# Feed forward stage with ternary weights stationary for gate and up, and the inner layer left untransposed

## The chip, the cores and the metric

One core of a Trainium2 chip runs the whole program. The metric is the device time of one execution in microseconds, which lasts as long as that core is at work. TensorE (PE in the rows, its weight loads PEld), VectorE (DVE), ScalarE (ACT), GpSimd (POOL) and SyncE (SP, which here only issues DMAs) each work through their own list of instructions in order and meet at semaphores.

## The reference

1600 tokens (16 sequences of 100) of 512 values go through one block: cross attention (16 heads of 128, 361 context positions of 256 values), then a feed forward layer with 1.58 bit weights. The diff touches only the second half:

```
x = x + xattn(layernorm(x), ctx)                # its last product, with Wo, is done in the third stage
n = layernorm(x)
h_bitlinear(a, w) = act_quant(fwht(a)) @ weight_quant(w).T
  fwht:         normalised Walsh-Hadamard transform along the last axis
  act_quant:    s = 127 / max|row|;  clip(round(a * s), -128, 127) / s
  weight_quant: s = mean|w|;         clip(round(w / s), -1, 1) * s
x = x + h_bitlinear(silu(h_bitlinear(n, w_gate)) * h_bitlinear(n, w_up), w_down)
```

w_gate and w_up are 2048 x 512, w_down is 512 x 2048. The inner layer of a token has 2048 values, and its Hadamard transform has that length.

## The kernel before

Three stages run one after the other: `queries`, `attention` and `feed_forward`. The first two leave the attention's output, transposed, in DRAM (`o_dram`). The third, which is all that changes, goes over the tokens in tiles of 128: 12 whole tiles and one of 64 (`TILES` is 13). Each engine has a list `step(i)`, written out by hand, and `pipeline` runs it for i = -2 to 12. A step works on several tiles at once: the down product of tile i, the inner layer of tile i+1, the output projection and the norm of tile i+2, and the loads and first projections of tile i+3.

For one tile t the data goes this way:

- SyncE's `load_o` (L1349) brings the attention output of the tile into the single buffer `o_in`, transposed, 1024 KB. `load_x` (L1361) brings the residual into the single buffer `x_in`; it waits for the sum x1 of the tile before. In step i SyncE issues, in this order: the two DMA transposes of q2 (`turn_q2`), load_x(i+3), load_o(i+4), and the store of the result (`store`).
- `high_o` (ScalarE, L1682) rounds o_in to the matmul's format, and `low_o` (GpSimd, L1428) makes the remainder. `out_proj` (TensorE, L1491) multiplies them with Wo: 16 heads, three matmuls each (high x high, high x low, low x high), 512 columns. AHEAD = 6 heads of a tile are done in the step before, the other 10 behind gate and up.
- `residual` (VectorE, L1811 to L1818) adds x, giving x1, and takes mean and variance; `inverse_deviation` (GpSimd) makes the power; `norm` and `rotate_halves` (L1824, L1832) follow. `norm_T` transposes into psA, `high_xT` (ScalarE, L1709) and `low_xT` (VectorE, L1836) split it, and `rotate_in` (TensorE, L1513) multiplies with a 256 x 256 Hadamard matrix, giving token rows in psF.
- `scales1` takes the maximum of the rows, `round1` and `ints1` make 8 bit integers, `q1_T` (L1524) transposes them, and `copy_q1T` (L1729) brings them to SBUF.
- `gate_up(t, j)` for four blocks j of 512 inner values: q1T is the stationary operand, the 8 bit ternary weights `wt` are the moving one, 512 columns at a time (L1542), so that the tokens are on the partitions. Silu (ScalarE, L1743) takes gate's scale as its per-partition scale, and `hidden` (VectorE, L1898) multiplies with up and its scale.
- The Hadamard transform of the 2048 inner values is partly done with sums and differences, on VectorE (L1907, L1914, L1920) and on GpSimd (L1447, L1450, L1456), within `hid` and `half_rot`. The rest takes a Hadamard matrix of 256: `hidden_T` (TensorE, L1588) transposes each block, `high_hT` (ScalarE, L1689) and `low_hT` (VectorE, L1801) split it out of PSUM, and `rotate_hidden` (L1598) multiplies.
- `peak`, `scales2`, `round2` and `ints2` make the integers q2, a DMA turns them, and `down` (L1608) gives psF, which `scale_down` (ScalarE, L1735) scales and `result` (GpSimd, L1461) adds to x1.

In `step`, ScalarE's order behind the four Silus is high_hT 0 and 1, high_o(i+3), scale_down(i), high_hT 2 and 3, high_xT(i+2), round1, round2, copy_q1T, round2. VectorE's is residual(i+2), low_hT 0, norm, rotation, low_hT 1, peak 0 and so on. GpSimd's is rotate_pair0, rotate_across, inverse_deviation, low_o(i+3), result(i), move_residuals. The half tile has versions of its own (`gate_up_halves`, `hidden_T_halves`, `cross_halves`), and TensorE fills pauses with matmuls that nobody reads (`busy`, L1616).

Of the kernel before, what the change touches and what calls it, by code (L numbers as in the profile page):

```python
# [14 lines left out]
F32 = mybir.dt.float32  # L15
# [38 lines left out]
def build(nc, x, ctxT, ctx_k, wq, wk, wv, wo, gq, gk, w_ff, ident_in, had_in, out):  # L54
# [4 lines left out]
    with ExitStack() as top:  # L59
# [10 lines left out]
        passed = {e: sem(e + "_passed") for e in ("sp", "act", "dve", "pe")}  # L70
# [1183 lines left out]
def feed_forward(nc, sbt, sem, passed, bank0, ident, neg_half, w127, o_in, d_stored, d_first, x, x_in, xT0, wo_hi, wo_lo, had_in, o_dram,  # L1254
# [10 lines left out]
    with ExitStack() as ctx:  # L1265
# [13 lines left out]
        al, ald = sb("al", [P, 2]), sb("ald", [P, 1])  # L1279
# [21 lines left out]
        p_out, p_xT, p_rx, p_q1T, p_gu, p_hT, p_rh, p_down = (  # L1301
            s(f"p3_{n}") for n in ("out", "xT", "rx", "q1T", "gu", "hT", "rh", "down"))
# [5 lines left out]
        a_q1T, a_sil, v_h, g_pair0, v_pair1, v_r2, g_r2 = (s(n) for n in ("a3_q1T", "a3_sil", "v3_h", "g3_pair0", "v3_pair1",  # L1308
                                                                                  "v3_r2", "g3_r2"))
        v_cross, a_half = s("v3_cross"), s("a3_half")  # L1310
# [4 lines left out]
        AHEAD, FIRST = 6, 10  # L1315
# [22 lines left out]
        def _(sp):  # L1338
# [78 lines left out]
        def _(pool):  # L1417
# [22 lines left out]
            def rotate_pair0(t):  # L1440

                pool.wait_ge(v_h, t * NB + 2)
                if due(t * NB):
                    pool.wait_ge(p_hT, t * NB)
# [7 lines left out]
            def rotate_across(t):  # L1452
# [3 lines left out]
                nc.gpsimd.tensor_tensor(half_rot[:, 2:4, :], hid[:, 0:2, :], hid[:, 2:4, :], op=ALU.subtract).then_inc(g_r2, 1)  # L1456

            def result(t):
                pool.wait_ge(a_y, t + 1)
                pool.wait_ge(g_old, (t + 2) * 2)  # L1460
                nc.gpsimd.tensor_tensor(y[:], y[:], x1[:, 0, :], op=ALU.add).then_inc(g_y, 1)  # L1461

            def step(i):
                if real(i + 1) and not last_tile(i + 1):
# [4 lines left out]
                if real(i + 3) and not (isinstance(i, int) and i == -2):  # L1469
                    low_o(i + 3)  # L1470
# [8 lines left out]
        def _(pe):  # L1479
            def out_proj(t, heads):  # L1480
                first = isinstance(t, int) and t == 1
                if heads[0] == 0:
                    if not first:
                        pe.wait_ge(g_o, t - 1)
                        pe.wait_ge(v_xT, t - 1)
                for h in heads:
                    if first:
                        pe.wait_ge(v_o, h // OH + 1)
# [6 lines left out]

            def norm_T(t):
                pe.wait_ge(v_xr, t * 2)
                for c in range(DC):
                    last = nc.tensor.transpose(psA[:, c * P:(c + 1) * P], xr[:, c * P:(c + 1) * P], ident[:])
# [17 lines left out]
            def q1_T(t):  # L1517
# [3 lines left out]
                if due(t * NB):  # L1521
                    pe.wait_ge(v_hT, t * NB)
                for c in range(DC):
                    last = nc.tensor.transpose(psTb[1][:, c * P:(c + 1) * P], q1[:, c * P:(c + 1) * P], ident_b[:])  # L1524
                last.then_inc(p_q1T, 1)

            def gate_up(t, j):
# [18 lines left out]
            def gate_up_halves(t, j):  # L1546

                if j == 0:
                    pe.wait_ge(a_q1T, t + 1)
                pe.wait_ge(a_mag[1], 2 * t - 1 + j)  # L1550
                pe.wait_ge(v_h, t * NB + j - 1)
                apart(pe, pe_passed)
                for k in range(2):
                    for c in range(DC):
                        for g in range(2):
                            col = (j + g * NB // 2) * DIM
                            last = nc.tensor.matmul(psB[g * TH:(g + 1) * TH, 2 * j + k, :], q1T[:, c, g * TH:(g + 1) * TH],  # L1557
                                                    wt[:, k, c, col:col + DIM], start=(c == 0), stop=(c == DC - 1),
                                                    tile_position=(0, g * TH))
                last.then_inc(p_gu, 1)  # L1560

            def hidden_T_halves(t, n):
                pe.wait_ge(v_pair1, t * 6 + 5 + n)
                pe.wait_ge(a_q1T, t + 1)
                for c in range(DC):
                    last = nc.tensor.transpose(psT[n][:, c * P:(c + 1) * P], hid[:, n, c * P:(c + 1) * P], ident[:])  # L1566
                last.then_inc(p_hT, 1)
# [11 lines left out]

            def hidden_T(t, n):  # L1580
                if n % 2 == 0:
                    pe.wait_ge(g_r2 if n else v_r2, t + 1)
                if n < 2:
                    pe.wait_ge(a_q1T, t + 1)
                else:
                    pe.wait_ge(v_hT, t * NB + n - 1)
# [470 lines left out]
```

## Time and profile before

| | us |
|---|---|
| three runs: median (lowest, highest) | 1415.81 (1414.24, 1416.08) |
| the profiled execution: span | 1415.7 |
| TensorE busy in the span | 1384.3 (98%) |
| VectorE, ScalarE, GpSimd busy | 933.8 (66%), 940.2 (66%), 517.2 (37%) |
| one step of the third stage, first gate/up matmul to the next | 29.14 |

The span runs from the first instruction to the last of one profiled execution. Busy time is the time for which an engine had an instruction under way; TensorE's matmuls overlap, so the distance between the starts of two matmuls tells what one costs, not its length. The third stage begins at about 1029 us of the span.

### The profile page before, as it was taken

The page shows a single profiled execution, that of the slowest core. Times are in us where ns is not written, and L with a number is a line of the kernel's source. Part 1 is how long each engine was busy: PE and PEld are TensorE (multiplying, and loading weights), DVE is VectorE, ACT ScalarE, POOL GpSimd, SP SyncE. Part 2 cuts the span into 40 slices and gives each one's busy share as a digit, 9 for nine tenths or more (in the row PEclk, how much of TensorE's full clock was granted, in tenths as well). Part 3 has the DMA queues.
Part 4 walks back from the last instruction along what each step waited for, and adds up shares of the span by engine and source line. Part 5 has one row for each costly group of instructions (what it writes and reads, how often), then busy time and mean ns, then how long its engine had stood idle before and what let it go on. Part 6 is the DMA issues. An engine that isn't in the chain of part 4 may idle for free. (4 is left out here: it accounts for less than half of the span.)

```text
span 1415.7 us, 25806 instructions
## 1 busy us (share of the span) xinstructions
PE 1384.3 (98%) x8407; PEld 1192.2 (84%) x8407; DVE 933.8 (66%) x2399; ACT 940.2 (66%) x2072; POOL 517.2 (37%) x323
## 2 busy tenths in 40 slices
PE   8999988999999999999999999999989999999998
PEld 8889867999999999999999999998867677776775
DVE  5222036667777777777777777766457677776775
ACT  4566558888888888888888888887533433343332
POOL 0033324432233223332323332324645465655551
PEclk9999999999999999999999999999989999999999
DMA  6867823334443443444344344325443322233211
GB/s 219 215 189 220 226 54 91 100 111 117 128 112 114 134 128 114 116 124 134 107 124 117 113 133 128 106 82 172 126 153 79 86 60 67 61 97 75 60 30 42
DMA packets 173492, 165.05 MB, mean 117 GB/s; under 512 B 81440, under 2 KB 149040, under 8 KB 171568
## 3 DMA queue, kind: packets, MB, share of 16 engines
q1 hardware_dynamic: 166448, 150.82, 38.5%
q10 hardware_dynamic: 6912, 12.59, 2.7%
q8 instruction: 69, 1.13, 0.3%
q14 instruction: 63, 0.52, 0.1%
HBM read 123.44 MB, written 33.01 MB: 111 GB/s over the span
## 5 line engine op out<-in xcount | busy, mean ns | idle before, releaser
L764 POOL TENSOR_TENSOR rk_sp<-ms_sp,neg_half 76x10 f32<-76x10 f32 (+1 forms) x128 | 238.5, 1880 | 567.0 <-DMA ms_sp<-ms 567.0
L1194 DVE CUSTOM_DVE_ANT_0 sc<-psS,rk 100x361 f32<-100x361 f32 x256 | 136.4, 533 | 97.1 <-PE psS L839 71.3
L986 ACT ACTIVATE pr<-ex,ri 100x361 f32<-100x361 f32 x256 | 153.6, 600 | 63.6 <-DVE ri L1184 63.6
L979 ACT ACTIVATE ex<-sc,nb,rq_all 100x361 f32<-100x361 f32 x256 | 175.9, 687 | 7.8 <-DVE nb L1203 7.8
L867 PE MATMUL psZ<-pT_hi,cK_hi 120*128 120x400 f32 (+1 forms) x384 | 133.3, 347 | 0.0
L867 PE MATMUL psZ<-pT_hi,cK_lo 120*128 120x400 f32 (+1 forms) x384 | 132.4, 345 | 0.0
L867 PE MATMUL psZ<-pT_lo,cK_hi 120*128 120x400 f32 (+1 forms) x384 | 132.2, 344 | 0.0
L852 PEld LDWEIGHTS psP<-ident,pr 100*120 100x120 f32 (+1 forms) x768 | 80.2, 165 | 43.5 <-issue 35.3
L839 PE MATMUL psS<-ring_hi,q_hi 128*100 128x362 f32 x256 | 97.0, 379 | 5.0 <-DVE mx L1194 5.0
L852 PE MATMUL psP<-ident,pr 100*120 100x100 f32 (+1 forms) x768 | 96.5, 261 | 4.0 <-ACT pr L986 4.0
L1176 DVE TENSOR_TENSOR pT_lo<-psP,pT_hi 121x600 fp32r<-121x600 f32 x128 | 99.0, 773 | 1.5 <-ACT pT_hi L1010 1.5
L882 PE MATMUL psNV<-z,wv_sb 128*128 128x200 f32 x504 | 97.2, 336 | 0.8 <-issue 0.8
L1184 DVE RECIPROCAL ri<-rs 100x1 f32<-100x1 f32 x256 | 41.3, 161 | 85.5 <-ACT ex L979 81.5
L1689 ACT ACTIVATE hT_hi<-psT 128x512 fp32r<-128x512 f32 x48 | 27.5, 596 | 99.8 <-PE psT L1588 99.8
L961 ACT ACTIVATE ring_hi<-bank 128x362 fp32r<-128x362 f32 x128 | 60.6, 473 | 44.1 <-PE bank L815 42.6
L1542 PE MATMUL psB<-wt,q1T 128*128 128x512 fp8e4 x384 | 86.6, 379 | 0.0
L815 PE MATMUL bank<-cT_hi,wk_hi 128*128 128x362 f32 x256 | 85.3, 333 | 1.0 <-DVE ring_lo L1129 1.0
L815 PE MATMUL psK<-cT_hi,wk_hi 128*128 128x362 f32 x256 | 85.0, 332 | 0.7 <-DVE ring_lo L1129 0.7
L1010 ACT ACTIVATE pT_hi<-psP 121x600 fp32r<-121x600 f32 x128 | 84.7, 662 | 0.0
L882 PEld LDWEIGHTS psNV<-z,wv_sb 128*128 128x128 f32 x504 | 83.0, 190 | 1.2 <-issue 1.1
L839 PE MATMUL psS<-ring_hi,q_lo 128*100 128x362 f32 x256 | 84.0, 328 | 0.0
L839 PE MATMUL psS<-ring_lo,q_hi 128*100 128x362 f32 x256 | 83.9, 328 | 0.0
(295 smaller groups left out, 3947.6 us busy)
## 6 DMA issues: line engine op xcount, KB each, us to landing
rk<-rk_dram SPq DMA_DIRECT2D x64, 564.1 KB
q_dram<-q_out SPq DMA_DIRECT2D x64, 200.0 KB, 4.3
q_in<-q_dram SPq DMA_DIRECT2D x64, 200.0 KB, 5.2
o_dram<-o SPq DMA_DIRECT2D x64, 200.0 KB, 5.4
stage<-in_w_ff SPq DMA_DIRECT2D x12, 1024.0 KB, 6.3
w_in<-in_w_ff ACTq DMA_DIRECT2D x48, 256.0 KB, 2.4
o_in<-o_dram SPq DMA_DIRECT2D x12, 1024.0 KB, 5.9
cT_in<-in_ctxT SPq DMA_DIRECT2D x15, 361.0 KB, 5.4
```

The lines of the kernel that those rows point to most:

```text
L764: nc.gpsimd.tensor_tensor(rk_sp[:, cols], ms_sp[:, cols], neg_half[0:HG * SKR, :].to_broadcast([HG * SKR, n]), op=ALU.pow).then_inc(g_rk, 1)
L815: last = nc.tensor.matmul(psK[h % 2][:, 0:SKP], w[:, c, col:col + D], x[:, slot, c, :], start=(n == 0), stop=(n == 3 * CC - 1))
L839: last = nc.tensor.matmul(psS[0:SQ, 0:SKP], w[:, u % 2, cols], x[:, u % NG, h, :], start=(i == 0), stop=(i == 2))
L852: last = nc.tensor.transpose(psP[0:KW[i], k, i * SQ:(i + 1) * SQ], pr[:, 2 * half + k, KO[i]:KO[i] + KW[i]], ident[0:SQ, 0:SQ])
L867: last = nc.tensor.matmul(psZ[c][:, 0:UQ], w[0:KW[i], b % 2, i, c * P:(c + 1) * P], x[0:KW[i], u % 2, i, :], start=(n == 0), stop=(n == 8))
L882: last = nc.tensor.matmul(bank[:, k * 2 * SQ:(k + 1) * 2 * SQ], wv_sb[:, c, col:col + D], z[:, first % 4:first % 4 + 2, c, h * SQ:(h + 1) ...
L979: nc.scalar.activation(ex[:, h % 2, :], sc[:, h % 2, :], ACT.Exp, bias=nb[:, h % 2:h % 2 + 1], scale=factor(n), accum_out=rs[:, h % 2:h % ...
L986: nc.scalar.activation(pr[:, h, :], ex[:, h % 2, :], ACT.Copy, scale=ri[:, h % 2:h % 2 + 1]).then_inc(a_pr, 1)
L1010: nc.scalar.activation(two_heads(pT_hi, u, half), psP[0:KW[0], :, 0:3 * SQ].rearrange("p k (i q) -> p k i q", q=SQ), ACT.Copy).then_inc(a_ ...
L1176: nc.vector.tensor_tensor(two_heads(pT_lo, u, half), psP[0:KW[0], :, 0:3 * SQ].rearrange("p k (i q) -> p k i q", q=SQ), two_heads(pT_hi, u ...
L1194: nc.vector.tensor_tensor_reduce(out=sc[:, h % 2, :], in0=psS[0:SQ, 0:SK], in1=rk[:, u % 2, h, :], scale=1.0, scalar=-3.0e38, op0=ALU.mult ...
L1542: last = nc.tensor.matmul(psB[:, 2 * (j % 2) + k, :], q1T[:, c, :], wt[:, k, c, j * DIM:(j + 1) * DIM], start=(c == 0), stop=(c == DC - 1))
```

## The change

Gate and up are computed with the ternary weights as the stationary operand, in pieces of 128 x 128, and the transposed integers q1T as the moving one, 128 columns at a time. The inner values come out on the partitions and the tokens along the columns, so `hidden_T` and its halves version go away, and high_hT and low_hT read `half_rot` in SBUF. Gate's scale is now one per column: `scales1` spreads it over a row of 128 (`al_rows`), TensorE transposes that (`al_T`), ScalarE copies it (`copy_alT`), and VectorE multiplies each gate block with it (`gate`) ahead of Silu. Up's scale is put off to `scales2`. The head products are split into `out_high` (both high parts, 10 heads ahead of time) and `out_low`, and low_o moves from the end of a step of GpSimd (tile i+3) to the start of the next (tile i+2). SyncE loads o for tile i+3 instead of i+4. All waits of the passing marks share one semaphore.

```diff
@@ sync, step
-            load_o(3, 3 * TT)
...
                 if real(i + 3):
                     load_x(held(sp, i + 3), held(sp, start(i + 3)))
-                if real(i + 4):
-                    load_o(held(sp, i + 4), held(sp, start(i + 4)))
+                if real(i + 3):
+                    load_o(held(sp, i + 3), held(sp, start(i + 3)))
                 store(i, held(sp, start(i)))
@@ gpsimd
             def low_o(t):
                 pool.wait_ge(a_o, t + (NO - 1))
-                pool.wait_ge(v_xr, 2 * t - 2)
+                pool.wait_ge(v_q[1], 2 * t - 2)
...
-                nc.gpsimd.tensor_tensor(half_rot[:, 2:4, :], hid[:, 0:2, :], hid[:, 2:4, :], op=ALU.subtract).then_inc(g_r2, 1)
+                for n in range(2):
+                    nc.gpsimd.tensor_tensor(half_rot[:, 2 + n, :], hid[:, n, :], hid[:, 2 + n, :], op=ALU.subtract).then_inc(g_r2, 1)
             def result(t):
                 pool.wait_ge(a_y, t + 1)
+                pool.wait_ge(v_hT, t * NB + (NB + NB // 2 if isinstance(t, int) and t == TILES - 2 else 2 * NB))
...
             def step(i):
+                if real(i + 2) and not (isinstance(i, int) and i < 0):
+                    low_o(i + 2)
                 if real(i + 1) and not last_tile(i + 1):
                     rotate_pair0(i + 1)
                     rotate_across(i + 1)
                 if real(i + 2) and i > -2:
                     inverse_deviation(i + 2)
-                if real(i + 3) and not (isinstance(i, int) and i == -2):
-                    low_o(i + 3)
@@ tensor
+            def out_high(t, heads):
+                if heads[0] == 0:
+                    pe.wait_ge(a_o, t + (NO - 1))
+                    pe.wait_ge(v_x1, t - 1)
+                for h in heads:
+                    for w in (wo_hi, wo_lo):
+                        nc.tensor.matmul(psA[:], o_hi[:, h, :], w[h // HALF][:, h % HALF, :], ...)
+            def out_low(t):
+                pe.wait_ge(g_o, t - 1)
+                for h in range(H):
+                    last = nc.tensor.matmul(psA[:], o_lo[:, h, :], wo_hi[h // HALF][:, h % HALF, :], ...)
+                last.then_inc(p_out, 1)
+            def al_T(t):
+                pe.wait_ge(v_scale[0], 6 * t + 6)
+                nc.tensor.transpose(psT[0][:, 0:TT], al_rows[:], ident[:]).then_inc(p_alT, 1)
@@ gate_up
-                for k in range(2):
-                    for c in range(DC):
-                        last = nc.tensor.matmul(psB[:, 2 * (j % 2) + k, :], q1T[:, c, :],
-                                                wt[:, k, c, j * DIM:(j + 1) * DIM], start=(c == 0), stop=(c == DC - 1))
-                last.then_inc(p_gu, 1)
+                width, chunks = (TH, FC // 2) if last_tile(t) else (TT, FC // NB)
+                for k, done in enumerate((p_gate, p_up)):
+                    for i in range(chunks):
+                        col = (j * chunks + i) * P
+                        for c in range(DC):
+                            last = nc.tensor.matmul(psB[:, 2 * (j % 2) + k, i * width:(i + 1) * width], wt[:, k, c, col:col + P],
+                                                    q1T[:, c, 0:width], start=(c == 0), stop=(c == DC - 1))
+                    last.then_inc(done, 1)
@@ tensor, step behind gate and up (hidden_T gone)
+                    out_high(i + 2, range(AHEAD, H))          # AHEAD = 10
+                    out_low(i + 2)
                     down(i, 0, front)
                     down(i, 1, front)
+                    rotate_hidden(i + 1, 0), (1), (2)
                     norm_T(i + 2)
                     rotate_hidden(i + 1, 3)
+                    out_high(i + 3, range(0, 1))
                     rotate_in(i + 2)
+                    out_high(i + 3, range(1, 7))
                     q1_T(i + 2)
+                    al_T(i + 2)
+                    out_high(i + 3, range(7, AHEAD))
@@ scalar, step
+                    silu(i + 1, j)                             # for each j; in place in sil
+                    high_hT(i + 1, n)                          # all four, from half_rot
                     high_o(i + 3)
                     scale_down(i)
                     high_xT(i + 2)
                     round1(i + 2); round2(i + 1, 0); copy_q1T(i + 2)
+                    copy_alT(i + 2)
                     round2(i + 1, 1)
@@ vector
+            def gate(t, j):
+                dve.wait_ge(p_gate, t * NB + j + 1)
+                dve.wait_ge(a_alT, t + 1)
+                nc.vector.tensor_tensor(sil[:, j % 2, :], psB[:, 2 * (j % 2), :], alT (repeated), ALU.mult).then_inc(v_g, 1)
             def hidden(t, j):
-                nc.vector.scalar_tensor_tensor(hid[:, j, :], psB[:, 2 * (j % 2) + 1, :], al[:, 1:2], sil[:, j % 2, :], ...)
+                nc.vector.tensor_tensor(hid[:, j, :], psB[:, 2 * (j % 2) + 1, :], sil[:, j % 2, :], ALU.mult).then_inc(v_h, 1)
@@ vector, step
+                    gate(n), hidden(n) for n in 0, 1, 2; gate(3), rotate_within(2), hidden(3), rotate_within(3)
+                    low_hT(0); residual(i + 2); low_hT(1); low_hT(2); norm; rotate_halves; low_hT(3); peak(0); low_xT(i + 2)
+                    peak(1), peak(2), peak(3); scales1(i + 2); scales2(i + 1)
```

## Rows read from the trace of the kernel before

**Rows 1.** The page, busy time of each engine and granted clock in 40 slices

```profile
PE 1384.3 (98%) x8407; PEld 1192.2 (84%) x8407; DVE 933.8 (66%) x2399; ACT 940.2 (66%) x2072; POOL 517.2 (37%) x323
...
PEclk9999999999999999999999999999989999999999
```

**Rows 2.** Groups of TensorE in 960 to 1416: busy us, mean ns, idle before

```profile
L1542 PE MATMUL psB<-wt,q1T 128*128 128x512 fp8e4 x384 | 86.6, 379 | 0.0
...
L1588 PE MATMUL psT<-ident,stage 128*128 128x128 f32 x192 | 28.1, 281 | 2.5 <-DVE stage L1920 2.5
```

**Rows 3.** TensorE in order of time, one step: start us, length us

```profile
1157.07 7.22 PE L1542 MATMUL psB<-wt,q1T 128*128 128x512 fp8e4 x32
1163.94 0.58 PE L1491 MATMUL bank<-wk_hi,o_hi 128*128 128x512 f32 x1
...
1171.12 1.03 PE L1588 MATMUL psT<-ident,stage 128*128 128x128 f32 x8
1171.99 3.62 PE L1608 MATMUL psF<-wt,q2T 128*128 128x512 fp8e4 x16
...
1184.52 0.40 PE L1524 MATMUL psT<-ident_b,q 128*128 128x128 bf16 x4
...
1186.21 7.22 PE L1542 MATMUL psB<-wt,q1T 128*128 128x512 fp8e4 x32
```

**Rows 4.** Busy time of each engine in one step

```profile
1157.07:1186.21 29.14, 29.11 (x161) 20.61 (x161) 21.35 (x40) 11.32 (x16) 16.31 (x10) 1.00 0.29 73
```

**Rows 5.** VectorE in order of time, the step from 1186.21

```profile
1186.68 0.69 DVE L1876 TENSOR_SCALAR q<-mag 128x1024 bf16<-128x1024 f32 x1 [0.80 <-ACT mag L1721]
...
1192.51 0.75 DVE L1898 SCALAR_TENSOR_TENSOR stage<-psB,al,sil 128x512 f32<-128x512 f32 x1 [1.11 <-ACT sil L1743]
1193.30 2.40 DVE L1907 TENSOR_TENSOR stage<-stage 128x256 f32<-128x256 f32 x2
...
1198.84 1.23 DVE L1920 TENSOR_TENSOR stage<-stage 128x1024 f32<-128x1024 f32 x1
1200.45 0.69 DVE L1811 TENSOR_TENSOR x<-bank,x_in 128x512 f32<-128x512 f32 x1 [0.39 <-PE bank L1491]
```

**Rows 6.** SyncE in order of time, the same step

```profile
1201.17 0.34 SPq L1361 DMA_DIRECT2D x_in<-in_x  x1
1209.20 0.37 SPq L1349 DMA_DIRECT2D o_in<-o_dram  x1
```

**Rows 7.** The loads of o, issue to landing, 1100 to 1300

```profile
DMA to landing us min/median/max: 5.8/5.9/6.0
```

**Rows 8.** ScalarE in order of time, the conversion of o

```profile
1201.86 1.91 ACT L1682 ACTIVATE o_hi<-o_in 128x2048 fp32r<-128x2048 f32 x1
```

**Rows 9.** Line L1524: ns min/median/max, first and last start

```profile
L1524 PE MATMUL psT<-ident_b,q x52: 219/219/230, 1039.1 to 1388.7; 128*128 128x128 bf16 x52
```

**Rows 10.** Line L1783

```profile
L1783 ACT ACTIVATE o_hi<-o_in x4: 611/616/632, 1028.9 to 1030.5; 128x512 fp32r<-128x512 f32 x4
```

**Rows 11.** Line L1907

```profile
L1907 DVE TENSOR_TENSOR stage<-stage x52: 409/740/1509, 1047.3 to 1395.4; 128x256 f32<-128x256 f32 x52
```

**Rows 12.** Line L1447

```profile
L1447 POOL TENSOR_TENSOR stage<-stage x24: 1264/1272/1289, 1045.6 to 1367.6; 128x512 f32<-128x512 f32 x24
```

**Rows 13.** Busy time and granted clock at the stage's start

```profile
1027.30:1030.60 3.30, 1.42 (x5) 0.93 (x6) 1.38 (x2) 2.28 (x6) 1.62 (x2) 1.00 0.40 122
1030.60:1034.00 3.40, 3.40 (x12) 2.86 (x12) 2.21 (x5) 2.01 (x4) 0.77 (x2) 0.50 0.97 321
1051.10:1054.50 3.40, 0.88 (x6) 0.45 (x5) 3.33 (x6) 0.00 (x0) 1.53 (x1) 1.00 0.00 0
1054.50:1061.30 6.80, 6.08 (x30) 5.67 (x29) 5.08 (x11) 3.59 (x4) 5.26 (x3) 0.50 0.12 39
```

**Rows 14.** TensorE in order of time, the last tile

```profile
1389.83 3.64 PE L1557 MATMUL psB<-wt,q1T 128*64 128x512 fp8e4 x32 [0.87 <-ACT q1T L1729]
...
1400.13 0.38 PE L1598 MATMUL psB<-had,hT_hi 128*128 128x256 f32 x1 [0.49 <-DVE hT_lo L1941]
```

More of the change, by code:

```diff
@@ L1300, in feed_forward @@
         a_o, v_o, g_o = s("a3_o"), s("v3_o"), s("g3_o")
-        p_out, p_xT, p_rx, p_q1T, p_gu, p_hT, p_rh, p_down = (
-            s(f"p3_{n}") for n in ("out", "xT", "rx", "q1T", "gu", "hT", "rh", "down"))
+        p_out, p_xT, p_rx, p_q1T, p_alT, p_gate, p_up, p_rh, p_down = (
+            s(f"p3_{n}") for n in ("out", "xT", "rx", "q1T", "alT", "gate", "up", "rh", "down"))
         v_x1, v_st, g_rs, v_xn, v_xr = (s(n) for n in ("v3_x1", "v3_st", "g3_rs", "v3_xn", "v3_xr"))
@@ L1479, in _, with first_out_proj @@
         def _(pe):
[L1480 to L1485, printed above, removed]
+            def first_out_proj(heads):
                 for h in heads:
-                    if first:
-                        pe.wait_ge(v_o, h // OH + 1)
+                    pe.wait_ge(v_o, h // OH + 1)
                     hi, lo = (w[h // HALF][:, h % HALF, :] for w in (wo_hi, wo_lo))
@@ L1494, in out_proj @@
                     last.then_inc(p_out, 1)
+            def out_high(t, heads):
[4 more added lines that the diff above has]
+                    for w in (wo_hi, wo_lo):
+                        nc.tensor.matmul(psA[:], o_hi[:, h, :], w[h // HALF][:, h % HALF, :],
+                                         start=(h == 0 and w is wo_hi), stop=False)
+            def out_low(t):
+                pe.wait_ge(g_o, t - 1)
+                for h in range(H):
+                    last = nc.tensor.matmul(psA[:], o_lo[:, h, :], wo_hi[h // HALF][:, h % HALF, :],
+                                            start=False, stop=(h == H - 1))
+                last.then_inc(p_out, 1)
             def norm_T(t):
                 pe.wait_ge(v_xr, t * 2)
+                pe.wait_ge(a_alT, t)
                 for c in range(DC):
-                    last = nc.tensor.transpose(psA[:, c * P:(c + 1) * P], xr[:, c * P:(c + 1) * P], ident[:])
+                    last = nc.tensor.transpose(psT[0][:, c * P:(c + 1) * P], xr[:, c * P:(c + 1) * P], ident[:])
                 last.then_inc(p_xT, 1)
@@ L1578, in down_halves @@
                 last.then_inc(p_down, 1)
[L1580 to L1586, printed above, removed]
-                for c in range(DC):
-                    last = nc.tensor.transpose(psT[n % 2][:, c * P:(c + 1) * P], half_rot[:, n, c * P:(c + 1) * P], ident[:])
-                last.then_inc(p_hT, 1)
             def rotate_hidden(t, n):
@@ L1644, in step @@
                         gate_up(i + 1, j)
-                if real(i + 2):
-                    out_proj(i + 2, range(FIRST if isinstance(i, int) and i == -1 else AHEAD, H))
-                if real(i + 1):
-                    hidden_T(i + 1, 0)
-                    hidden_T(i + 1, 1)
+                if isinstance(i, int) and i == -1:
+                    first_out_proj(range(FIRST, H))
+                elif real(i + 2):
+                    out_high(i + 2, range(AHEAD, H))
+                    out_low(i + 2)
                 if real(i):
@@ L1684, in high_hT @@
             def high_hT(t, n):
-                act.wait_ge(p_hT, t * NB + n + 1)
+                if last_tile(t):
+                    act.wait_ge(v_r2, t + 2)
+                else:
+                    act.wait_ge(g_r2, 2 * t + (n - 1)) if n >= 2 else act.wait_ge(v_r2, t + 1)
                 if n == 0:
@@ L1708, in high_xT @@
                     act.wait_ge(p_rx, t)
[L1709 removed]
+                nc.scalar.activation(xT_hi[:].rearrange("p c t -> p (c t)"), psT[0][:], ACT.Copy).then_inc(a_xT, 1)
             def round1(t):
[L1712 removed]
+                act.wait_ge(v_scale[0], 6 * t + 4)
                 if due(t):
@@ L1966, in step @@
                 if i == TILES - 2:
+                    gate(i + 1, 0)
                     hidden(i + 1, 0)
+                    gate(i + 1, 1)
                     rotate_within(i + 1, 0)
@@ L1983, in step @@
                     for n in range(3):
+                        gate(i + 1, n)
                         hidden(i + 1, n)
+                    gate(i + 1, 3)
                     rotate_within(i + 1, 2)
@@ L1999, in step @@
                     return
+                if real(i + 1):
+                    low_hT(i + 1, 0)
                 if real(i + 2):
@@ L2002, in step @@
                 if real(i + 1):
-                    low_hT(i + 1, 0)
+                    low_hT(i + 1, 1)
+                    low_hT(i + 1, 2)
                 if real(i + 2):
@@ L2015, in step @@
                 if real(i + 1):
-                    peak(i + 1, 2)
-                    peak(i + 1, 3)
+                    for n in range(1, NB):
+                        peak(i + 1, n)
                 if real(i + 2):
```

219 lines of the change are left out of this document (90 added, 129 removed).

## The prediction

> **What bounds the kernel now.** I read first the head of the page: TensorE is busy 98% of the span, at full clock almost throughout [rows 1]. Then the groups by line over the last third, the feed forward stage, since the diff touches only that stage: TensorE's matmul groups there show no idle time ahead of them but for 2.5 us once, and the transposes of the inner layer, L1588, are 192 matmuls, 16 for each of 12 tiles [rows 2]. Then TensorE in order of time over one step of the tile loop [rows 3]: its first gate/up matmul starts at 1157.07 and again at 1186.21, so a step takes 29.14 us. TensorE is busy 29.11 of it [rows 4], so the stage is bound by TensorE. Below, "+t" is the time in a step after its first gate/up matmul.
>
> How much room the others have decides this change. In the same row VectorE is busy 21.35, ScalarE 11.32, GpSimd 16.31. VectorE's landmarks [rows 5], against the step that starts at 1186.21: the rotation across blocks ends at +13.9, the residual sum x1 runs +14.2 to +14.9. SyncE [rows 6] issues x_in at +15.0 (it waits for x1) and o_in at +23.0. An o_in takes 5.9 us from issue to landing [rows 7], so it is there at about +28.9; the conversion that reads it, o_hi on ScalarE, 1.91 long [rows 8], runs at +15.7 of the NEXT step. It is a load with 16 us to spare.
>
> **The change, part by part.**
>
> TensorE's own work. Out go 16 transposes a step at L1588; eight of them take 1171.12 to 1171.99, 0.109 each [rows 3], so 1.74. Gate and up keep their 16384 moving columns, now as 128 matmuls of 128 columns instead of 32 of 512. The old ones pass in 6.87 [rows 3]. No row shows an 8 bit stationary operand. Nearest is L1524, a bf16 128x128 stationary with 128 columns: four end 0.40 after the first starts [rows 3], one lasts 0.219 [rows 9], so (0.40-0.22)/3 = 0.060 apart; a quarter of the old 0.215 is 0.054. I take 0.056, so 7.15, +0.28. The upper end is the f32 transposes' 0.109, so 13.95, +7.1. Below 0.054 nothing can be had, since the columns alone take that. The transpose of the scales adds one at 0.109. The head matmuls are the same 48, in another order. If nothing waited: 29.14-1.74+0.28+0.11 = 27.8 a step.
>
> The Trainium skill's page TensorE: Matmul & The Clock Gate, section Back-to-back issue gap, says that a real stream of weight load and matmul pairs at 128 columns runs at about 81 ns a pair, not at 56. No run of 128 such pairs is in this trace. By that rule gate and up would take 10.4, an estimate from the page.
>
> VectorE. Gate's scale now lies along the columns, so each block gets a multiply out of PSUM before Silu: 4 x 0.69 (x1, L1811, is the same shape and kinds of operand [rows 5]). The up product loses its scalar: 0.75 to 0.69, -0.24. The scale rows, 128 elements: +0.2. Together +2.7: 24.1 a step. Within a block the chain is now gate multiply 0.69, Silu 0.62 (the 512 element o_hi copy from SBUF, L1783 [rows 10]), up product 0.69: 2.0 a block, and it runs once for each of four blocks, since VectorE's next gate multiply is behind the up product. VectorE gets to the first one at +1.25, behind the integers of the tile before it (L1876, 1186.68 and 0.69 long, [rows 5]). So three blocks are done at 7.3 and the fourth gate multiply at +7.9; in before, the third product ended at +7.05. From there the order is the old one: 2.2 for the first half rotation beside GpSimd, 0.6 product, 1.2, 1.2 and 1.2, the rotation across ends at +14.3, half a microsecond later than now. TensorE doesn't feel that: it comes to the rotation of block 0 at 7.15+2.96 (12 high head matmuls)+3.73 (16 low ones)+3.45 (down) = +17.3.
>
> low_hT now reads two operands from SBUF. L1907, the half rotation of 256 elements, takes 0.41 at best and 1.51 at worst [rows 11], and its long pair, 2.40, lies beside GpSimd's work [rows 5]: I read it as each waiting till the other's instruction ends. GpSimd's cross subtraction, now two instructions of 512 elements at 1.27 [rows 12], starts with VectorE's at +13.1, and the first ends at +15.4. So: ScalarE's hT_hi ends at +15.0, low_hT of block 0 is held till +15.4 and ends at +16.1. It stands ahead of the residual in the new order, so x1 ends at +16.7, 1.8 later than now. If it were not held and the chain were short, x1's floor is the end of the low head matmuls, +14.0, plus 0.7.
>
> **The step I think decides: o_in.** low_o of GpSimd moves from the end of a step to the start of the next, and with it SyncE's load of o goes from tile i+4 to tile i+3, behind load_x, in the same step in which ScalarE's high_o(i+3) reads it. load_x waits for x1. So x1 +16.7, x_in's issue 0.35, o_in issued at +17.1, landed 5.9 later at +23.0, where 28.9 was good before. Behind high_o's wait on ScalarE stand: the scaling of down, xT_hi, both roundings and the copy of q1T. Nothing of them may pass. I walk on, with 0.6 for a pass over 512 elements on ScalarE [rows 10] and 0.7 on VectorE [rows 5]: high_o 1.91, ends +24.9; scaling 0.6, +25.5; xT_hi 0.6, +26.0; low_xT on VectorE 0.7, +26.7; rotate_in on TensorE 0.95 and 0.2 to arrive, +27.9; the peaks 1 to 3, queued behind low_xT, end at +28.5; the maximum and the scale 1.2, +29.7; round1 0.7, +30.4; VectorE finishes the second scale and makes the integers, +31.0; q1's transposes 0.2, the copy behind the first round2, +32.2; TensorE has by then three heads to finish, till +32.8. So a step takes 32.8. Walked with the same rules, the old order gives 29.0 and x1's end at +14.95, which is what the trace has (29.14, +14.9); so the walk is good to 0.2.
>
> TensorE then stands still where it waits for high_o (+21.9 to +24.9, 3.0), for low_xT (1.35), and for q1 (0.6), together 5.0; it does 27.8 of work. Cost without anything else: 32.8-29.1 = 3.7 in each of the ten steps 0 to 9 that convert an o tile behind a load: +37.
>
> The clock. At the start of the stage TensorE was busy 1.42 of 3.30 us, and then the granted clock is 0.50 (1.2 GHz) for 3.4 us; later 0.88 of 3.40, and then it is 0.50 for 6.8 [rows 13]. Those are idle times of 1.9 and 2.5, and every new step has 3.0 and 1.35 within 5 us. In each new step I expect a half clock stretch of 3.4 us, in rotate_in and the head matmuls behind it: half of it, 1.7, is lost, less the 0.4 or so of the 0.6 pause that it fills: +1.3 a step, +13. If the stretch is 6.8: 3.4 less 0.6, +28. None: 0.
>
> The rest. The step before the loop (gate and up of tile 0) had a pause of 2.5; it loses the transposes but TensorE now waits at the rotation, which starts at about +16.1 against +16.3: 0, +-2. Step 10 has no o load: -1.3. The last tile: 128 matmuls of 64 columns against 32 in 3.64 now [rows 14]; two gate multiplies (1.4) go in, the transposes, the copies and the PSUM sums between go out for quarter sums of 1.5 and 1.3; the rotation can start at about +10.4 against +10.3 now [rows 14]. 0, up to +2. The query and attention stages run the same instructions: 0. One shared semaphore for the passing marks costs nothing, since nobody waits on it.
>
> Sum: the profiled execution's time is its span, 1415.7, against a median of 1415.8. 1415.7+37+13-1.3 = 1464.
>
> **Rivals.**
> (a) The load binds but the clock holds, or x1 comes earlier. 1415.7+37-1 = 1452; with x1 at its floor of +14.7 each step is 2.0 shorter, 1432. For it: the pauses are split. Against: rows 13 show a fall after 1.9 alone. 25%.
> (b) Stationary loads don't keep up with 128 columns. At 0.109 gate and up end at +13.95; walking on gives a step of 37.7, 1415.7+10x8.5+5 (the other two steps and the last tile) = 1506: 6%. Half way between 0.056 and 0.109, at 0.082, the step is 34.2, with ten times 5.1 and 7 for the other three: 1473: 7%. For both: only four such pairs in a row are in the trace. Against: they were 0.060 apart. The half way case is about what the Trainium skill's TensorE: Matmul & The Clock Gate, section Back-to-back issue gap, has as the rule (81 ns).
> (c) VectorE's two-input instructions are held more than I walked, each low_hT once by 1.3 of GpSimd: x1 1.3 later, blocks 1 to 3 later: 1475. For: L1907's 1.51. Against: the result's new wait keeps GpSimd off. 7%.
> (d) The other side, faster. If o_in were ready, the walk gives 28.5 (VectorE's chain through x and q1 ends last, 0.7 over TensorE's 27.8): 11 x -0.6 = 1409; without that chain 11 x -1.37 = 1401. It decides from the point where o_in lands by about +19.3: a landing in 2.2 us instead of 5.9, or an issue before +13.4, ahead of the end of the head matmuls, which load_x forbids. The loads of the steady steps took 5.8 to 6.0 [rows 7]. 5%.
> (e) Gains and losses cancel, within 0.2%, which is about what a measurement here tells from nothing: 3%.
> (f) My own case, with the clock falling in most steps: 47%.
>
> Together: faster 0.05, same 0.03, slower 0.92. Range: (a) without its floor, (f) with 6.8 us stretches in half the steps, (c) and half of (b): 1440 to 1486.
>
> **What would show it.** In the changed kernel's trace: the first gate/up matmuls of two steps 33 to 34 apart; gate and up in 7.2; o_in issued near +17 and landed near +23, and high_o right behind it, named as the releaser of a TensorE pause of about 3; x1 ending near +16.7; granted clock of 0.50 once a step; GpSimd's result waiting till +25. Wrong if o_in's issue is not tied to x1, if high_o has no idle time ahead of it, if gate/up matmuls are 0.08 or more apart, or if steps take less than 29.

## The result, and the profile after

The changed kernel takes 1473.4 us (median; 1472.6 to 1477.8) beside 1415.1 for the kernel before on the same chip: a ratio of 1.042, interval [1.041, 1.043]. The profiled execution took 1473.3, its span is 1471.5.

The page, engines' busy time and the slices of TensorE's busy share and clock, against [rows 1]:

```profile
PE 1392.0 (95%) x9468; PEld 1235.6 (84%) x9468; DVE 961.8 (65%) x2462; ACT 941.5 (64%) x2083; POOL 526.6 (36%) x335
...
PE   8999989999999999999999999998888888888887
...
PEclk9999999999999999999999999999899999999999
```

TensorE's busy time rose by only 8 us, the span by 56; its share fell from 98% to 95%, and the slices in which it fell are all at the end, in the feed forward stage. (The page's own chain says little here: it reaches back only through the last tile. The waits have to be read by window.)

The first gate/up matmul of each tile gives the steps. They were 29.1 us long [rows 3]; now they start at 1037.2, 1067.1, 1102.3, 1136.8, 1171.6, 1207.7, 1242.4, 1276.8, 1311.1, 1345.2, 1379.3, 1416.4 and 1444.8. The ten steps that convert an o tile behind its load take 35.1, 34.5, 34.8, 36.1, 34.7, 34.5, 34.3, 34.1, 34.2 and 37.1, together 57.9 more than ten old ones. The rest is small: the step before them +0.56, the one behind them -0.35, the last tile +0.8, and the stages ahead of this one -3.1. The change doesn't touch those stages, and they differ by more than that from one execution to the next: in the profiled executions of e1 to e9 below, this stage starts anywhere from 1035.1 to 1045.5 (before's had a stretch at half clock at 13.5 us). Sum: +55.8, which is the difference of the spans, 1471.5 - 1415.7.

The groups of TensorE in 980 to 1474, against [rows 2]; behind the bar busy us, mean ns, and the idle time ahead with what ended it:

```profile
L1565 PE MATMUL psB<-q1T,wt 128*128 128x128 bf16 (+1 forms) x1664 | 92.6, 217 | 0.8 <-ACT q1T L1713 0.8
L1587 PE MATMUL psB<-had,hT_hi 128*128 128x256 f32 x200 | 55.7, 312 | 10.1 <-DVE hT_lo L1778 10.1
...
L1497 PE MATMUL bank<-wk_hi,o_hi 128*128 128x512 f32 x88 | 46.2, 525 | 32.8 <-ACT o_hi L1670 32.8
...
L1526 PE MATMUL psF<-had,xT_hi 128*128 128x256 f32 x48 | 19.9, 422 | 8.1 <-DVE xT_lo L1812 8.1
```

From the first gate/up matmul on, TensorE's idle times come to 54 us, where before has 5.7, and 33 of them end with o_hi. The mean of L1497 with wk_hi, 525 ns, where the same matmuls with ring_hi take 403, is already the second effect: many of them run at half clock. (The mean of L1565, 217, is a matmul's length from end to end of the array, not its distance from the next.)

Who waits for whom, 1040 to 1430 (us in total, times, longest):

```profile
POOL y L1461 <- ACT y L1719: 72.0, 10, 9.1
...
ACT o_hi L1670 <- DMA o_in<-o_dram: 57.1, 10, 7.6
...
PE bank L1497 <- ACT o_hi L1670: 32.8, 10, 5.2
...
PE psB L1587 <- DVE hT_lo L1778: 8.0, 12, 4.2
PE psF L1526 <- DVE xT_lo L1812: 7.8, 10, 1.1
```

Ten times, once in each long step, ScalarE waits for the o tile, and TensorE for ScalarE.

One such step in order of time, from 1207.68, put together from the engines' timelines. TensorE, against [rows 3]:

```profile
1207.68 7.39 PE L1565 MATMUL psB<-q1T,wt 128*128 128x128 bf16 x128
...
1221.40 3.63 PE L1597 MATMUL psF<-wt,q2T 128*128 128x512 fp8e4 x16
...
1226.30 0.39 PE L1587 MATMUL psB<-had,hT_hi 128*128 128x256 f32 x1 [0.32 <-DVE hT_lo L1778]
...
1232.78 0.79 PE L1497 MATMUL bank<-wk_hi,o_hi 128*128 128x512 f32 x1 [2.80 <-ACT o_hi L1670]
...
1234.57 0.58 PE L1526 MATMUL psF<-had,xT_hi 128*128 128x256 f32 x1 [0.57 <-DVE xT_lo L1812]
1234.95 0.41 PE L1526 MATMUL psF<-had,xT_lo 128*128 128x256 f32 x1
```

VectorE, against [rows 5]:

```profile
1222.82 0.98 DVE L1778 TENSOR_TENSOR hT_lo<-stage,hT_hi 128x512 fp32r<-128x512 f32 x1 [0.70 <-ACT hT_hi L1680]
1223.72 0.68 DVE L1787 TENSOR_TENSOR x<-bank,x_in 128x512 f32<-128x512 f32 x1
```

SyncE, against [rows 6], and the landings of six o loads, against [rows 7]:

```profile
1224.43 0.34 SPq L1360 DMA_DIRECT2D x_in<-in_x  x1
1224.87 0.38 SPq L1348 DMA_DIRECT2D o_in<-o_dram  x1
```

```profile
DMA to landing us min/median/max: 5.9/6.0/7.0
```

ScalarE and GpSimd, against [rows 8]:

```profile
1230.81 1.91 ACT L1670 ACTIVATE o_hi<-o_in 128x2048 fp32r<-128x2048 f32 x1 [5.22 <-DMA o_in<-o_dram]
```

```profile
1233.38 1.27 POOL L1461 TENSOR_TENSOR y<-y,x 128x512 f32<-128x512 f32 x1 [6.73 <-ACT y L1719]
```

Read it from the VectorE row on: low_hT of block 0 is 0.98 long where the others take 0.68 (GpSimd's instruction that writes half_rot runs beside it until +15.6; I read it as held by that), x1 ends at +16.7, x_in and behind it o_in are issued at +16.7 and +17.2, o_hi starts at +23.1 and ends at +25.0, TensorE goes on at +25.1 after a pause of 2.8, and GpSimd's result has waited 6.7 for the scaling behind o_hi.

The busy time of this step, of the pause, and of what follows it (PE, PEld, DVE, ACT, POOL, granted clock), against [rows 4]:

```profile
1207.68:1242.40 34.72, 31.03 (x243) 25.06 (x243) 23.55 (x45) 11.52 (x17) 17.22 (x11) 0.90 0.24 59
...
1232.60:1239.40 6.80, 6.05 (x17) 4.69 (x18) 5.00 (x16) 2.22 (x5) 2.50 (x3) 0.50 0.10 39
```

The granted clock is 0.50, the lower of its two levels, for 6.8 us from the end of the pause. So the pause is paid twice: 2.8 us of standing still, and then rotate_in and the head matmuls at half speed.

### The profile page after: what moved, and what is told of

Read it like the earlier page. It is cut to its first block and busy times, and to the rows that moved or that the text cites. A ratio compares the mean times of both kernels' runs of the same rounds, so it can differ in the third digit from the quotient of the medians.

```text
span 1471.5 us, 28072 instructions
## 1 busy us (share of the span) xinstructions
PE 1392.0 (95%) x9468; PEld 1235.6 (84%) x9468; DVE 961.8 (65%) x2462; ACT 941.5 (64%) x2083; POOL 526.6 (36%) x335
## 5 line engine op out<-in xcount | busy, mean ns | idle before, releaser
L1565 PEld LDWEIGHTS psB<-q1T,wt 128*128 128x128 fp8e4 x1664 | 89.8, 98 | 5.0 <-issue 4.2
L1565 PE MATMUL psB<-q1T,wt 128*128 128x128 bf16 (+1 forms) x1664 | 92.6, 217 | 0.8 <-ACT q1T L1713 0.8
L1680 ACT ACTIVATE hT_hi<-stage 128x512 fp32r<-128x512 f32 x50 | 29.9, 626 | 86.8 <-DVE stage L1913 69.8
L815 PE MATMUL psK<-cT_hi,wk_lo 128*128 128x362 f32 x256 | 83.9, 328 | 0.0
```

Of the source, the lines that this page charges most:

```text
L815: last = nc.tensor.matmul(psK[h % 2][:, 0:SKP], w[:, c, col:col + D], x[:, slot, c, :], start=(n == 0), stop=(n == 3 * CC - 1))
L1565: last = nc.tensor.matmul(psB[:, 2 * (j % 2) + k, i * width:(i + 1) * width], wt[:, k, c, col:col + P], q1T[:, c, 0:width], start=(c == 0) ...
```

## Experiments

"After" is the changed kernel. Each time stands beside the kernel before on the same chip: 1413.7 for the first four, 1414.9 for e5 to e7, 1415.1 for e8 and e9. The theory: the o load, whose issue now stands behind x1, sets the step, and the clock's fall behind its pause is a second, smaller price. The rivals: the new gate/up form or VectorE's longer work costs the time and the load is incidental.

**e1: the load of o ahead of the load of x, nothing else.**

```
 step(i) of SyncE, after:
-    load_x(i + 3)
     load_o(i + 3)
+    load_x(i + 3)
```

> The changed kernel with one pair of lines swapped: in SyncE's step the load of o stands ahead of load_x, so it waits only for low_o of the tile before (GpSimd, over at about +5.8 of a step) and no longer for the residual sum x1 (+16.6). Theory (the load of o, issued behind x1, is what lengthens the step): o_in is issued near +6, lands near +12, high_o runs right behind high_hT at +18 to +20, TensorE's pause of 3.9 us for o_hi goes, and with it the falls of the clock; the step goes from 34.9 to 28.5 us and the kernel to 1473-10x6.4 = 1409, a little faster than the kernel before (about 0.995). What ends last is then VectorE's chain to the integers of q1, with about 0.6 of pause at q1's transposes; at 27.8 (1402) TensorE alone would bind. Rival A (VectorE's extra 2.7 us of work and its waits for GpSimd's port use carry the loss): the step falls by less than 2 us, to 33 or more, and the kernel stays above 1450. Rival B (the stationary weights cost more than their rows say): gate and up stay long and the kernel stays above 1430.

Measured: 1413.0 us, ratio 0.9994 [0.9982, 1.0007]: all 58 us are gone (I had 1409), with 128 gate/up matmuls, the gate multiplies and the new orders of GpSimd and VectorE in place. SyncE in one step (from 1180.90), and the step's busy times:

```profile
1186.94 0.38 SPq L1348 DMA_DIRECT2D o_in<-o_dram  x1
1197.72 0.33 SPq L1360 DMA_DIRECT2D x_in<-in_x  x1
...
1198.80 1.90 ACT L1670 ACTIVATE o_hi<-o_in 128x2048 fp32r<-128x2048 f32 x1
```

```profile
1180.90:1209.90 29.00, 28.11 (x243) 22.95 (x243) 23.46 (x45) 11.39 (x17) 17.25 (x11) 1.00 0.30 74
```

o_in is issued at +6.0, and o_hi has no idle time ahead of it. The step is 28.96, a little above the 28.5 that I had for it. What is left is two short waits of TensorE in each step (1070 to 1380):

```profile
PE psT L1537 <- DVE q L1859: 5.4, 10, 0.6
...
PE psB L1587 <- DVE hT_lo L1778: 3.9, 11, 0.5
```

**e2: the old kernel with the late load alone.** No other part of the change is in it.

```
 SyncE, before:
-    load_o(3, 3 * TT)            # ahead of the loop
 step(i):
     load_x(i + 3)
-    load_o(i + 4)
+    load_o(i + 3)
```

> The kernel before with only SyncE's order of the change: o is loaded for tile i+3 behind load_x(i+3) instead of for tile i+4; nothing else is changed. Theory: this alone is worth as much as the whole change or more. x1 ends at +14.9, o_in is issued at +15.4, lands 7 later at +22.4, high_o ends at +24.3 and the second pair of high_hT stands behind it; low_o on GpSimd (4.6) follows it, and the first head matmuls of tile i+3 wait for low_o. A step of 33.5 at full clock, 35 to 36 with the falls of the clock, against 29.14: 1415+10x5.9 = 1474, between 1458 and 1486. Rival A (the other parts of the change carry the loss): within 10 us of the kernel before, under 1425.

Measured: 1469.0, ratio 1.038 [1.036, 1.041]. In the old kernel the load alone costs 55 us, where the whole change costs 58. SyncE and ScalarE in one step, from 1204.34 (x1 ends at +14.9):

```profile
1219.74 0.38 SPq L1349 DMA_DIRECT2D o_in<-o_dram  x1
...
1226.42 1.91 ACT L1681 ACTIVATE o_hi<-o_in 128x2048 fp32r<-128x2048 f32 x1 [6.32 <-DMA o_in<-o_dram]
```

It fits the theory and adds something: x1 is 1.8 earlier than in after and o_hi starts at +21.3 to +22.2 in nine of the ten steps, and yet the steps are as long (34.0 to 34.8 in eight of them). Those eight end 12.4 to 12.9 behind o_hi's start, where after has 10.8 to 12.0. The old order of ScalarE and TensorE puts more of the inner layer behind the wait.

**e3: after, with work for TensorE in the pause.** Fifteen matmuls that nobody reads, to hold the clock.

```
 step(i) of TensorE:
     rotate_hidden(i + 1, 3)
+    busy(psT[1], 15)
     out_high(i + 3, range(0, 1))
```

> The changed kernel with 15 matmuls that nobody reads (512 columns, 0.23 us each, 3.4 together) in TensorE's pause ahead of the first head matmuls of tile i+3. The wait is as long as before, the engine only isn't idle in it. Theory: the granted clock then stays at 2.4 GHz in the steps, rotate_in takes 0.95 instead of 1.9 and the head matmuls 0.23 instead of 0.43; the step goes from 34.9 to about 33.7, the kernel to 1473-12 = 1461 (1455 to 1466). Rival (the falls of the clock are hidden by the wait for the integers, which ends the pause at q1's transposes anyway): unchanged within 3 us. If the fillers run past the landing they cost: then above 1475.

Measured: 1464.4, ratio 1.035 [1.033, 1.037]; the granted clock is 1.00 throughout a step, and the step 33.2:

```profile
1202.70:1235.80 33.10, 31.57 (x257) 25.68 (x256) 23.46 (x45) 11.31 (x17) 17.23 (x11) 1.00 0.30 65
```

```profile
1224.87 3.59 PE L1605 MATMUL psT<-wk_hi 128*128 128x512 f32 x15
```

(I had 33.7 for the step and 1461 in all.) Its steps give the cleanest rule of the case. In nine steps from 1068.8 on, o_hi starts at +23.21, 23.27, 24.06, 23.34, 23.14, 23.15, 23.07, 23.26, 23.22 in a step and the steps are 33.20, 33.28, 34.07, 33.34, 33.14, 33.17, 33.09, 33.27, 33.23: with the clock held, a step is o_hi's start and 10.0. (The walk had +23.0 and 32.8, so 9.8.) Ten steps come to 336.1, against 349.3 in after: the clock costs 13 of the 58 us. The median fell by only 9: the filling also runs in the step before the loop, where nothing has to be filled (32.4 for 29.9), and the profiled execution, 1461.8, was the fastest of four.

**e4: after, with x1 ahead of low_hT of block 0 on VectorE.**

```
-    low_hT(i + 1, 0)
     residual(i + 2)
+    low_hT(i + 1, 0)
```

> The changed kernel with residual(i+2) ahead of low_hT(i+1, 0) on VectorE. x1 then ends at +15.0 to +15.2 instead of +16.6, and x_in and o_in are issued 1.5 earlier. Theory (the step is a loop through x1 and the load): the step gets shorter by about the same 1.5 us, less what the clock makes of it, and the kernel goes to 1473-15 = 1458 (1453 to 1466). Rival A (the rotation of block 0, which waits for low_hT(0) and now comes 1.5 later, sets the step): unchanged or slower. Rival B (the load's own time isn't bound to x1): unchanged.

Measured: 1450.4, ratio 1.025 [1.023, 1.027]. One step, from 1131.13, with x1 ending at +15.1:

```profile
1145.55 0.68 DVE L1787 TENSOR_TENSOR x<-bank,x_in 128x512 f32<-128x512 f32 x1
...
1146.71 0.41 SPq L1348 DMA_DIRECT2D o_in<-o_dram  x1
...
1153.49 1.91 ACT L1670 ACTIVATE o_hi<-o_in 128x2048 fp32r<-128x2048 f32 x1 [4.83 <-DMA o_in<-o_dram]
```

More than I expected (23 us, not 7 to 20): the nine steps ahead of the last are 31.4 to 33.5, and in six of them the clock falls, in three it doesn't. x1's place counts as long as the load hangs on it.

**e6: after, o ahead of x but still behind x1**, so that only x_in's 0.43 us on the queue is taken away.

```
 step(i) of SyncE, after:
+    sp.wait_ge(v_x1, i + 2)
+    load_o(i + 3)
     load_x(i + 3)
-    load_o(i + 3)
```

> The changed kernel with the load of o still behind x1 but issued ahead of load_x instead of behind it (a wait for x1 stands ahead of both). Theory (o_in landed 7.0 us after its issue and not 5.9, since x_in is moved at the same time just ahead of it, and its issue itself took 1.4 instead of 0.4): o_in lands 0.4 (x_in's issue) and 1.1 earlier, near +22.5 of a step instead of +24.0; the step gets 1.5 shorter, the kernel 1473-15 = 1458 (1453 to 1466). Rival (the landing is slower for another reason, the step's other traffic): only the 0.4 is won, 1469.

Measured: 1469.4, ratio 1.037 [1.035, 1.040]. My number was 1458; the rival's 1469 held. o_hi does start 0.5 earlier (+22.7 in most steps), but half of the steps are 34.1 to 34.3 as in after: in six steps the clock's fall lasts 6.8 us, and such a step is o_hi's start and 11.4 to 11.7. So the wait for x1 is what makes e1's gain, not the order of the two loads.

**e7: e1 without the gate multiplies.** Silu reads gate unscaled out of PSUM, so the scale of gate is left out of the result.

```
-    gate(i + 1, n)                                       # VectorE, four a tile
-    nc.scalar.activation(sil[:, j % 2, :], sil[:, j % 2, :], ACT.Silu)
+    nc.scalar.activation(sil[:, j % 2, :], psB[:, 2 * (j % 2), :], ACT.Silu)
     # ... and the waits of Silu and copy_alT that belong to them
```

> The kernel with the load of o ahead of load_x (step 28.96) and without VectorE's four multiplies of gate with its scales: Silu reads the gate block out of PSUM unscaled, so the result is not the reference's. It asks where the 1.4 us of a step that TensorE no longer works (16 transposes less, 0.4 more for gate and up and the scales) went. Theory (into VectorE's chain, whose end, the integers of q1, TensorE waits for: four multiplies of 0.6 and the wait for them ahead of Silu): x1 ends about 1.5 earlier, the pauses ahead of the rotations and q1's transposes go, the step goes to 28.0 and the kernel to 1413-9 = 1404 (1401 to 1407). Rival (the step is held by the waits for GpSimd's instructions or by gate and up themselves): 28.8 or more, above 1410.

Measured: 1412.1, ratio 0.998 [0.996, 0.999]; a step 28.83 against 28.96. I had 28.0 and 1404: this theory fell. But the run takes less from VectorE than its edit says. The four multiplies were 2.7 us a step; VectorE's busy time fell only from 23.46 to 22.65, and x1 ends at +16.65 instead of +16.8. The half rotations (L1900), which now start at +6.3 instead of +7.9 and lie beside GpSimd's own rotations throughout, took 5.0 us a step instead of 3.5. The line in e1 and in e7 (ns min/median/max, 1070 to 1380):

```profile
L1900 DVE TENSOR_TENSOR stage<-stage x44: 410/793/1518, 1072.8 to 1366.2; 128x256 f32<-128x256 f32 x44
```

```profile
L1900 DVE TENSOR_TENSOR stage<-stage x44: 799/1346/1517, 1080.9 to 1373.1; 128x256 f32<-128x256 f32 x44
```

So e7 doesn't tell what a lighter VectorE would bring; it tells that the gate multiplies cost next to nothing where they stand. The wait ahead of q1's transposes is what it was (1070 to 1380):

```profile
PE psT L1537 <- DVE q L1859: 5.9, 11, 0.5
```

It ends a chain that begins with TensorE itself: rotate_in, maximum, scale, round1, integers, 3.3 to 3.4 us, against the matmuls of six heads, 2.7 us, that lie beside it. Some 0.4 of the chain is VectorE's order: in e1's step from 1180.9 the last matmul of rotate_in ends at +23.9, and the maximum of its result starts at +24.4, right behind three peaks of the inner layer.

**e5: e1, with x1 first, and one head more ahead of q1's transposes.**

```
 TensorE:  out_high(i + 3, range(1, 8)); q1_T; al_T; out_high(i + 3, range(8, AHEAD))
 VectorE:  residual(i + 2); low_hT(i + 1, 0)
 SyncE:    load_o(i + 3); load_x(i + 3)
```

> An attempt at a better kernel: the load of o ahead of load_x, residual(i+2) ahead of low_hT(i+1, 0), and seven instead of six heads of tile i+3 ahead of q1's transposes, which TensorE waited 0.56 for. Theory: x1 ends at +15.1, the chain through the norm is about 0.5 earlier, the rotation of block 0 waits 0.5 for low_hT, and the pause at q1 is filled; a step of 28.6 against 28.96, the kernel at 1413-4 = 1409 (1405 to 1412), 0.3% under the kernel before. Rival (the rotation of block 0 now waits for longer than the integers are early): no gain or 1415 and more.

Measured: 1412.5, ratio 0.998 [0.996, 0.999], just outside the 1405 to 1412 that I had; steps 28.66 to 28.73. Both waits of e1 are gone:

```profile
1182.30:1211.00 28.70, 28.22 (x242) 22.72 (x241) 23.58 (x46) 11.38 (x18) 16.84 (x11) 1.00 0.30 75
```

```profile
PE psB L1565 <- DVE stage L1892: 2.0, 11, 0.2
```

This version beats the kernel before by 0.2%; from e1 (0.9994) the runs hardly tell it apart. TensorE is at its own bound again, 28.2 busy of 28.7, about 0.45 a step under the kernel before. Ten steps gain 4.6 by that, the step before them and the last tile take back 1.0, and 2.4 were measured.

**e8: e3 and e4 together** (x1 first, `busy(psT[1], 8)`), and **e9: e3 and e6 together** (o ahead of x behind x1, 13 filling matmuls): the same two edits with the clock held.

> The changed kernel with residual(i+2) ahead of low_hT(i+1, 0) and 8 unread matmuls (1.8 us) in the pause ahead of the first head matmuls, so that the clock should hold. Put beside the run with 15 fillers and the old order (a step of 33.2, 1464). Theory (the step is a loop through x1 and the load of o, and x1 sets it one to one): x1 ends 1.5 earlier, so the step is 31.7 and the kernel at 1464-15 = 1449, hardly better than the unfilled kernel with this order (1450), where the clock fell in only some of the steps. Rival (more than x1 moves the loop: the unfilled kernel gained 23 us, not 15, from the order): a step of 31 or less, under 1443.

> The changed kernel with the load of o issued ahead of load_x, still behind x1, and 13 unread matmuls (3.0 us) in the pause. Unfilled, that swap gained 4 us, and the steps of three kernels stood at 34.1 to 34.3 whatever the edit, with a fall of the clock in each. Theory (the falls of the clock, not the landing, set those steps to one length, and hid what the earlier issue brings): with the clock held the 0.4 us of x_in's issue show, a step of 32.8 instead of 33.2, 1464-4 = 1460. Rival (the landing waits for something else and the swap brings nothing): 33.2 and 1464.

Measured: e8 1447.4, ratio 1.022 [1.020, 1.024]; in the nine steps ahead of the last o_hi starts at +21.6 to +22.2 and the steps are 31.6 to 32.2. e9 1459.3, ratio 1.030 [1.028, 1.032]; there o_hi at +22.7 to +23.0, steps 32.7 to 33.0. In both, as in e3, every step but the last is o_hi's start and 10.0, to 0.1. With the clock held the step follows the load one to one. TensorE's waits in e9 (1040 to 1430), against those of after:

```profile
PE psF L1527 <- DVE xT_lo L1814: 8.0, 11, 1.1
PE psT L1538 <- DVE q L1861: 5.7, 10, 0.8
...
PE bank L1498 <- ACT o_hi L1672: 1.0, 1, 1.0
```

The wait for low_xT is as it was and the long one is filled. The wait ahead of q1's transposes, 5.7, is new against after (0.5 there): with the clock held the head matmuls are done before the integers come.

## Why the prediction was right

The forecast was 1464 within 1440 to 1486, and slower with 0.92; it came to 1473.4, 9 above. By the number alone two rivals were nearer, the half way case of (b) with 1473 and (c) with 1475; it is the trace that decides between them and mine. Step by step:

- **The mechanism** held in every link up to TensorE's pause, and e1 and e2 show it from both sides: away with the load's place, and nothing is left of the loss; the load's place alone, and nearly all of it is there. Rival (a) is out since the clock did fall, (b) by the spacing of the matmuls (56 ns), (c) by x1's end (+16.7), (d) and (e) by the load's landing.
- **Gate and up** pass in 7.2 us: 1171.56 to 1178.75 in one step, 56 ns a matmul over 128, where I had 7.15 from four in a row [rows 3, 9]. The 81 ns of the Trainium skill's page TensorE: Matmul & The Clock Gate, section Back-to-back issue gap, were not seen here: 128 pairs of weight load and matmul, 8 bit stationary and bf16 moving, ran at 56.
- **VectorE** has 23.5 us a step, where I had 24.1. low_hT of block 0 was longer once, by 0.3, and ended where I had it (+16.1), and x1 ended at +16.7, as forecast.
- **o_in**: issue +17.2 (+17.1), o_hi +23.1 to +25.0 (+23.0 to +24.9), TensorE's pause 2.8 (3.0). The walk was right to 0.1 up to here in the typical step. In three of the ten it was not: in the steps from 1136.8 and 1171.6 the load took 6.8 and 7.0 from its issue to o_hi, in the latter its issue alone 1.41; and in the last each load is two DMAs, so that o_in is issued later and in two pieces, o_hi waited 7.6 and TensorE 5.2. SyncE in that step, from 1379.3:

```profile
1396.10 1.20 SPq L1358 DMA_DIRECT2D x_in<-in_x  x2
1397.41 1.86 SPq L1346 DMA_DIRECT2D o_in<-o_dram  x2
```

- **The landing** is the term that was mis-sized: "o_in issued at +17.1, landed 5.9 later at +23.0" for all ten steps alike. o_hi starts at +23.48, 23.16, 24.00, 24.14, 23.13, 23.19, 23.12, 23.19, 23.29 and 25.53, together 6.2 later. The last of them alone makes 2.5, and I hadn't looked at it apart.
- **The walk behind it** (high_o, scaling, xT, peaks, scale, integers, q1T) had 9.8 and took 10.0 with the clock held (e3, e8, e9): 2.0 in ten steps.
- **The two short pauses** were not as walked. TensorE waited 0.6 to 1.1 for low_xT, not 1.35, and in the ten steps not at all for q1, where I had 0.6: the head matmuls at half clock filled that time.
- **The clock** cost what was forecast, by another way, so that the agreement is luck. Ten times o_hi's start and 10.0 come to 336.2, the steps to 349.3: 13.1, where I had 13. "In each new step I expect a half clock stretch of 3.4 us": there was one in each, but in seven of the ten of 6.8, the other value of [rows 13]. A step with 3.4 (from 1136.8, 1311.1 and 1345.2) is o_hi's start and 10.8 or 10.9, so 0.8 to 0.9 for the clock, not 1.3; one with 6.8 is 11.2 to 12.0, so 1.2 to 2.0, not the 2.8 that I had. Part of the slow work lies beside the chain through VectorE for which TensorE would have waited anyway (with the clock held, e3 has waits of 0.6 to 1.1 and 0.5 there). More steps with the long stretch and a lower price for each happened to give my sum.

6.2, 2.0 and 0.1 make the 8.3 us by which the ten steps (349.3) exceed ten times 34.1.

- **The rest**: step 10 gained 0.35, not 1.3; the last tile lost 0.8 (0 to 2), the step before the loop 0.56 (0, +-2); the stages ahead were 3.1 shorter, which no term of mine had and which is chance. The gain that rival (d) would have found, had o_in been ready, is in e1: 28.96 a step where I had 28.5. Of the 0.5 between, 0.3 is TensorE's own work, 28.1 busy against my 27.8, and 0.2 its waits: 0.35 for low_hT of block 1, which I had not counted, and 0.55 for q1, where I had 0.7. With both gone, TensorE's own bound is 28.2 busy in 28.7, against my 27.8 (e5).

What stays open: when a fall of the clock lasts 3.4 us and when 6.8. It decides 0.4 to 1 us a step, and with it why e6, whose load is earlier, is hardly shorter than after. (In the last of e6's steps it lasts 10.2.) In the steps of after and e6 that are 34.1 to 34.5 long and have 6.8, the fall begins at +24.1 to +24.7 each time, so that step and fall keep pace with each other; no run here tells what holds them together.

## What to carry to other kernels

When a buffer's last reader moves into the next step, the load that refills it moves too, and takes its place behind whatever its queue already waits for: follow the queue, not only the engine. Here the issue of the load hung on a late result of the same step, and its 6 us to landing stood in the step's longest chain. Issued ahead of the load that waits for that result, it gave back 58 us, and what the rest of the change is worth the runs can't tell from nothing (0.9994). The order of the two loads alone, with the wait kept (e6), gave back 4. And TensorE's pause of 3 us was paid more than once, since the work right behind it ran at half clock; matmuls that nobody reads were worth 9 us, with the pause left in place.

## What the runs showed of the hardware that I had not expected

- TensorE's granted clock fell to the lower level in every step of after, with idle times of 2.8 to 3.9 us (5.2 in the last) and 0.6 to 1.1, a pair of head matmuls between them. In e1, with 0.35 and 0.55, it never fell in the loop. In e4, with 1.4 to 2.4 and 1.05, it fell in six of the nine steps ahead of the last, and the idle times alone don't say in which: with 1.65 and 1.05 it fell in the step from 1195.9 and not in the one from 1164.4.
- Of two loads issued one behind the other on SyncE, the second one's issue may take long. In after it is o_in's, 0.37 to 0.38 in eight of the nine steps ahead of the last and 1.41 in one; in e6 it is x_in's, 1.63 to 2.40 in all nine, behind the 1 MB of o_in.
- VectorE's half rotations (256 elements, two inputs in SBUF) took 0.41 us at best and 1.52 at worst in e1. In the steps of e1 the short ones, 0.41, have no GpSimd instruction beside them. In those of e7 every one lies beside GpSimd's rotations and none is under 0.80, which ate 1.5 of the 2.7 us that had been taken out.
- Gate and up of the last tile, with 64 moving columns, take 1444.80 to 1448.6, 29 to 30 ns a matmul against 56 with 128 columns, with a weight load of 128 columns for each:

```profile
1444.80 3.89 PE L1565 MATMUL psB<-q1T,wt 128*128 128x64 bf16 x128 [0.76 <-ACT q1T L1713]
```

So the weight loads didn't bind even at half the columns; [rows 14] has 3.64 for the old form.
